# A fused layer on one core: another address pattern for DVE's normalise, an earlier start for GpSimd's adds

## The reference

```
xn  = layernorm(x)                              # (x - mean) / sqrt(var + 1e-5), over the 128 columns
q, k, v = xn@Wq, xn@Wk, xn@Wv                   # 16 heads of 8 columns
q, k = q/|q|, k/|k|                             # per head: the squares of 8 columns are summed
a   = softmax(8 * q k^T, causal) v              # per batch and head, 512 x 512
out = x + a@Wo + sum over the top 2 of 8 experts of gate * (gelu(xn@W1+b1)@W2 + b2)
```

## Time and profile before

| | |
|---|---|
| median of 3 runs | 843.71 us |
| the profiled execution | 836.56 us |
| its span, first to last instruction | 834.6 us |
| outside the span | 1.96 us |
| busy in the span: PE, DVE, ACT, POOL | 709.8, 525.5, 482.5, 437.9 us |
| granted clock of PE, mean | 0.924 |

### The profile page before, as it was taken

How to read it: one execution, slowest core, us unless ns; L and a number is a source line. 1 busy time by engine, 2 the same in 40 slices (tenths; PEclk the granted TensorE clock), 3 DMA queues, 4 the chain that set the end, 5 groups by cost and what they waited for, 6 DMA issues and landing times. The chain is left out here.

```text
span 834.6 us, 18970 instructions
## 1 busy us (share of the span) xinstructions
PE 709.8 (85%) x5959; PEld 438.2 (53%) x5959; DVE 525.5 (63%) x1350; ACT 482.5 (58%) x801; POOL 437.9 (52%) x558
## 2 busy tenths in 40 slices
PE   3877399999999788887899949788679999999986
PEld 2656123333333377786799939676568333333322
DVE  7699976888888623333344414443345689999964
ACT  2766368888888523332344413322234889888883
POOL 4455256777777743464300150445430777777773
PEclk9899579999999989999999969889989899999998
DMA  6886493444444544333222222222221445444441
GB/s 198 265 260 181 108 202 75 95 94 101 98 95 95 136 133 124 109 107 107 77 74 69 79 65 64 79 69 83 71 75 45 86 90 106 107 97 103 112 108 32
DMA packets 170228, 89.18 MB, mean 107 GB/s; under 512 B 77217, under 2 KB 159937, under 8 KB 170177
## 3 DMA queue, kind: packets, MB, share of 16 engines
q1 hardware_dynamic: 161984, 71.74, 34.4%
q0 software_dynamic: 8192, 16.79, 7.1%
HBM read 39.47 MB, written 32.24 MB: 86 GB/s over the span
## 5 line engine op out<-in xcount | busy, mean ns | idle before, releaser
L677 ACT ACTIVATE prob<-psum 128x1024 f32<-128x1024 f32 x320 | 312.6, 1027 | 60.9 <-PE psum L769 50.0
L687 ACT ACTIVATE prob<-psum,prob 128x256 f32<-128x256 f32 x284 | 116.3, 471 | 241.1 <-PE psum L908 153.2
L794 PE MATMUL psum<-prob,v 128*18 128x384 f32 (+2 forms) x2560 | 181.6, 393 | 2.7 <-DVE prob L1181 1.8
L920 PE MATMUL psum<-prob 128*128 128x128 f32 x1136 | 151.4, 287 | 30.1 <-ACT prob L687 15.8
L553 POOL DMA_INDIRECT rows<-slot_y,idx x128 | 123.8, 967 | 101.1 <-DVE acc L1234 65.0
L908 PE MATMUL psum<-xs,prob 128*128 128x256 f32 x568 | 149.8, 411 | 26.4 <-DVE xs L1311 22.7
L555 POOL DMA_INDIRECT slot_x<-rows,idx x128 | 128.4, 1003 | 76.6 <-DMA rows<-xn_rows 39.0
L920 PEld LDWEIGHTS psum<-prob 128*128 128x128 f32 x1136 | 146.6, 201 | 40.1 <-issue 17.7
L769 PE MATMUL psum<-qks 32*128 32x512 f16 (+3 forms) x1024 | 128.0, 309 | 17.7 <-DMA qks<-dup 8.1
L566 POOL TENSOR_SCALAR_AFFINE_SELECT prob<-prob 128x512 f32<-128x512 f32 x128 | 90.4, 706 | 96.0 <-ACT prob L677 95.2
L908 PEld LDWEIGHTS psum<-xs,prob 128*128 128x128 f32 x568 | 111.4, 207 | 45.6 <-issue 16.8
(11 more groups left out here) (141 smaller groups left out, 677.0 us busy)
## 6 DMA issues: line engine op xcount, KB each, us to landing
xs<-slot_x SPq DMA_DIRECT2D x71, 128.0 KB
slot_y<-xs SPq DMA_DIRECT2D x71, 128.0 KB
xs<-in_L_attn_x SPq DMA_DIRECT2D x16, 256.0 KB, 3.5
prob<-in_L_ffn_W SPq DMA_DIRECT2D x16, 256.0 KB, 3.4
xn_rows<-xns SPq DMA_DIRECT2D x16, 256.0 KB, 4.2
xn_cols<-xts SPq DMA_DIRECT2D x16, 256.0 KB, 4.2
xt<-xn_cols SPq DMA_DIRECT2D x16, 256.0 KB
rows<-xn_rows SPq DMA_DIRECT2D x16, 256.0 KB, 2.9
```

Of the source, the lines that this page charges most:

```text
L677: act.activation(prob[:, q % 2, KEPT[u], :], score[(q + u) % 2], ACT.Exp, scale=SCALE / UP ** 2).then_inc(exp_done, 1)
L687: act.activation(hs[:, s, c, :], psum[:, 2 * s + c // 2, (c % 2) * FT:(c % 2 + 1) * FT], ACT.Gelu, bias=ws[:, s, B1C + c:B1C + c + 1]).the ...
L794: mm = pe.matmul(ps_octet[w // 2][32 * g:32 * g + VW, first:first + cols], lhs, prob[:, w % 2, KEPT[u], c:c + cols], start=(i == 0 and not ...
L920: mm = pe.matmul(psum[:, 6 + s, j * D:(j + 1) * D], hs[:, s, c, j * P:(j + 1) * P], ws[:, s, W2C + c * D:W2C + (c + 1) * D], start=(c == 0 ...
```

## The change

Two edits. In `normalise` the input and the output of the `tensor_scalar` are read and written in another order: of the 128 columns of a tile first 0 and 64, then 1 and 65, and so on; as an address pattern that is 64 pairs with a step of 64 elements inside the pair, where it was one run of 128. Every element gets the same value at the same place. And `sum_squares(i)` waits for `rstd_ready` to reach 2i+5, the first reciprocal of `normalise(i+2)`, in place of `xn_ready` at 2i+6, its last `tensor_scalar`.

```diff
@@ sum_squares (GpSimd)
                 if not (known(i, NB // 2 - 2) or known(i, NB // 2 - 1)):
-                    count = counted_by(pool, 2 * i + 6)
-                    pool.wait_ge(xn_ready, count)
+                    count = counted_by(pool, 2 * i + 5)
+                    pool.wait_ge(rstd_ready, count)
@@ normalise (DVE)
+            def by_turns(ap):
+                return ap.rearrange("p (a d) -> p d a", a=2)
+
...
                     for t in range(TB):
-                        ins = dve.tensor_scalar(xns[:, s, t, :], xs[:, par, s, t, :], mv[:, s, t, 0:1],
-                                                rstd[:, s, t:t + 1], ALU.subtract, ALU.mult)
+                        ins = dve.tensor_scalar(by_turns(xns[:, s, t, :]), by_turns(xs[:, par, s, t, :]),
+                                                mv[:, s, t, 0:1], rstd[:, s, t:t + 1], ALU.subtract, ALU.mult)
```

## The result

The changed kernel takes 853.3 us in the median of 4 runs (850.57 to 856.04), the kernel before 843.0 in the 4 runs that go with them (838.81 to 844.35). The ratio is 1.0123, with an interval of 1.0085 to 1.0161: 10.4 us slower. The prediction was 855.8, in a range of 850 to 866, slower.

The account below looks back on a forecast made before the run. DVE was taken to set the pace of steps 4 to 7. The terms 13.6 + 2.5 + 1.5 - 5.6 - 0.5 + 0.6 gave +12.1 us on 843.7, so 855.8, range 850 to 866.

Parts of the forecast that it names:

- The mode stays: In `normalise`, `tensor_scalar` keeps handling two elements per clock under the new pattern and still collides with GpSimd; slower, chance 0.64.
- The rivals in which the pattern ends the mode: In `normalise`, one element per clock and no collision: 840.1 us, or 843.6 to 847 if the step costs more; chance 0.30.
- the sign of the mode: Undisturbed `tensor_scalar` in step 1: near 340 to 390 ns if two per clock stays, 405 or more if it ends.
- the second rival: In `normalise`, two per clock ends but the 64-element step costs 86 ns or more: 843.6 to 847 us; within the shared 0.30.
- DVE is held, GpSimd isn't: In `normalise`, one `tensor_scalar` gets through per GpSimd add, so DVE goes at GpSimd's pace while adds keep their duration.
- The rival in which GpSimd waits: Adds held off until the eighth `tensor_scalar`, selects collide as before, only 1.7 us added: 845.4 us; chance 0.06.
- All six adds lie on `normalise`, +3.35 us, and the selects are freed, -1.42: Per loop step, adds run from 41.3 to 46.4: `normalise` takes 5.7 us for 2.35, the select loses its 1.42 us collision.
- the prediction's own signs: Steps 4 to 7: `tensor_scalar` median near 1 us, `normalise` 5 to 6.5, lines 965 and 967 at 0.29, step 10 to 11.
- Step 2 and step 3: Early steps: +2.5 us for step 2; +1.5 for step 3, where three adds run during a wait for the store.
- Behind the last step: After the loop, the first three adds miss the select, 1.4 us of DVE; counted -0.5, as scores hang on SP's queue.
- The step of 64: The pattern's stride in `normalise`: 43 ns per `tensor_scalar`, mostly hidden, +0.6 us over all eight steps, bounds 0 and 5.
- The sum: All terms together: +12.1 us, with +5.2 from the low bounds and +25.8 from the high ones.

Follow-up runs that it names:

- The new order alone: The kernel before, with SP issuing the store of the normalised rows in front of the loads of x: 754.57 us, ratio 0.9945.
- the freed select alone: The kernel before, with GpSimd's long adds of both batches in front of the short ones, in two half-sum buffers: 845.93 us, ratio 0.9964.

## Why the prediction was right, and the step in it that was wrong

*The mode stays.* Right. The first `tensor_scalar` beside the adds take 1.48 us longer as a group of four (2.65 - 1.17), and the pattern alone keeps its pace of 0.26 us. The rivals in which the pattern ends the mode are out, and the broken pattern of three runs of 42 shows what would have followed: no collision, and 0.315 us of pace. The duration, which the prediction had named as the sign of the mode (340 to 390 ns if it stays, 405 or more if it ends), does not tell: it is 395 ns in both, and only the pace and the longest instruction differ. No run has the mode ended with a step of 64, so the price in the second rival stays untested. The Trainium skill, page "VectorE: DVE Perf Modes", section "Mode 2×_2P — use both read ports for one tensor", sets its condition on the outermost dimension, which has to be even, or odd and the same for input and output, and not on the step. By that rule 64 and 128 keep the mode and 3 against 126 ends it, and the traces agree: a longest instruction of 1460, 1190 and 405 ns.

*DVE is held, GpSimd isn't.* Right. In the changed kernel the long adds beside `normalise` take 1.27 us, once 1.31. The rival in which GpSimd waits is out.

*All six adds lie on `normalise`, +3.35 us, and the selects are freed, -1.42.* This is the step that failed, although the total came out, in "the adds would begin at 41.3 and end at 46.4". Two of the six lie there, +1.53, and no select up to step 6 is freed (1.34 and 0.66 in the loop). The adds were taken as one block, because they follow each other without a wait for DVE; the wait of the third for ACT's roots was not followed up to what releases it. With four `sums` buffers the predicted step came out as predicted (5.52 us against 5.7, the select at 0.29). The two errors nearly cancel: the sum had 13.6 for `normalise` in steps 4 to 7 and -5.6 for the selects of steps 3 to 6, where the trace has +6.14 and, but for 0.2 us in step 3, nothing. By the prediction's own signs it was wrong here: it named a median near 1 us, a `normalise` of 5 to 6.5 us, lines 965 and 967 at 0.29 and a step of 10 to 11 us. The changed kernel has a median of 0.397 us over all 64, a `normalise` of 3.9 (44.83 to 48.72), 1.34 and 0.66, and a step of 9.9.

*Step 2 and step 3.* +2.5 against +2.47, or 2.3 against the runs whose step 2 begins as late. It agrees though the road was another: the wait for the store is gone from DVE's timeline, and one for ACT's `std` of 2.42 us stands in its place. For step 3 the sum had +1.5 and -1.4 for its select, +0.1 in all, against +1.13. It counted on a wait for the store behind the reciprocal, in which three adds would run; there is no such wait, and the first two adds meet the first four `tensor_scalar` (2.66 us).

*Behind the last step.* -0.5 against +0.96. The prediction had it that SP's queue and GpSimd's last adds set this end, and that held (SP +10.97, DVE's memset +8.45). DVE did gain there: its last `normalise` ends 9.74 later and its memset 8.45, so 1.29 us less, near the 1.4 of the freed select. But that was worth nothing, and the prediction didn't count that GpSimd's chain gets longer: from the end of the last `normalise` to that of the last add it takes 20.57 us where it took 19.35.

*The step of 64.* +0.6 against nothing to be measured. The 43 ns per instruction were near (53 ns), but they lengthen the instruction and not its pace. A duration was taken for a cost on an engine whose instructions overlap.

*The sum.* +12.1 against +10.7 at the attention's start and +10.4 in the medians. The direction rests on the mechanism. The closeness is in part luck: errors of 7.5 and 5.6 us in the steps cancel to 1.9.

## What to carry to other kernels

When work is moved earlier on one engine, follow every wait in the block that moves, not only the first: the block may split, and then it meets the same neighbour again. Work on GpSimd does not become free beside DVE by moving it; it matters beside which kind of DVE instruction it lies. In this kernel an instruction of the select cost 1.05 us more beside the long add of 1.27, and 0.11 to 0.37 more beside the short ones of 0.61 and 0.40, while `bn_stats` took 1.64 us for eight with adds beside it and without. And ask of every freed microsecond what is late next: in this kernel it was the store behind two loads on SP. The new order alone gave a ratio of 0.9945, the freed select alone 0.9964, and both 0.9891.

## What the runs showed that I had not expected

The chips differ by more than any edit here: the kernel before took 843.9, 849.1 and 758.9 us in the medians of three sets. On the third chip the steps of the first part have the length they had on the others (8.33 us for step 4 with the new order alone, against 8.37). The difference is in the experts' part, 270.7 us from the first `ACTIVATE` of the kind of line 687 to the last, in place of 356.1 in the run with both long adds first on the second chip. TensorE's granted clock between 300 and 500 us was 0.98 there and 0.91 on the second chip, which is less than the difference. ACT's waits before that line which the profile puts down to `remote`, and whose source it doesn't name, sum to 66.1 us in that run on the second chip and to none on the third. What sets them was not tried and stays open. The ratio on the third chip therefore holds for a kernel whose rest is shorter: the 8.3 us that it stands for on 758.9 would be 1.0% of 843.
